# Inverse lengths and inverse roots moved from ScalarE and VectorE to a power on GpSimd, in the gate stage of a four-layer kernel

## The chip, the cores and the metric

The kernel runs on one core of a Trainium2 chip. The metric is device time in microseconds of one execution, in fp32. PE is TensorE, DVE VectorE, ACT ScalarE, POOL GpSimd, SP the engine that issues the transfers.

## The reference

The program is four layers of x = x + attention(n) * silu(gate(n)), with n the layer norm of x. The change touches the gate of layer 1, itself a small transformer of two layers on 2 x 1024 tokens of width 128, with 8 heads of 64 and a local window of 64 tokens:

```python
def l2norm(t):
    return t / jnp.clip(jnp.linalg.norm(t, axis=-1, keepdims=True), 1e-12)
...
def _layer(x, wqkv, qs, ksc, wo, lg, lb, w1, b1, w2, b2):
    h = shift_token(x)
    q, k, v = jnp.split(h @ wqkv, 3, axis=-1)
    ...
    q = l2norm(q) * qs
    k = l2norm(k) * ksc
    q, k = rotary_xpos(q, k)
    o = local_attention(q, k, v)
    ...
    x = x + o @ wo
    h = shift_token(x)
    mu = h.mean(-1, keepdims=True)
    var = h.var(-1, keepdims=True)
    h = (h - mu) / jnp.sqrt(var + 1e-05) * lg + lb
    h = h @ w1 + b1
    a, g = jnp.split(h, 2, axis=-1)
    h = a * jax.nn.gelu(g, approximate=False)
    x = x + h @ w2 + b2
    return x
```

The square roots in question are those of the lengths of q and k, one for each token and head, and of the variance, one for each token.

## The kernel before

The class TransformerGate treats the tokens in 8 units of 4 tiles of 128 tokens: units 0 to 3 are the first of the two layers, 4 to 7 the second. The work is cut into items, and `plan` puts each on a step: unit u has its attention on steps 8u to 8u+7, two steps to a tile, and its other items before and after. Inside a step the items stand by `rank`. Every engine walks the same list of items in that order and does its own part of each, so the list is the order of every engine's queue, and an instruction that waits holds up all that stands behind it on its engine.

What a unit does, by steps relative to its first: from -15 to -4 PE makes q, k and v (L1730); ACT squares q and k (L1910) and copies them (L1913), and DVE sums the squares of each head into F_ssq (L1964). At -7 `root` takes ACT's square root of F_ssq (L1865), and at -6 `lengths` runs `norms` on DVE (L2033 to L2039): two reciprocals and one refining step that turn 64 lengths of each token (4 tiles, q and k, 8 heads) into inverse lengths; for q, 8 times the inverse goes into the exponentials as a scale. From -8 to -1 POOL rotates the rows (`spin`, L2103 to L2108) in the order q0, q1, k0, k1, q2, k2, q3, k3; only the keys (L2103) need the inverse lengths first. From -4 to 2 PE turns each tile (`turn`, L1763), k and then q, and DVE copies the result (L2012, L2016); at step 2 POOL copies the last keys of the unit to the next one's place (L2081, or a memset at L2079), which in its queue stands between q1 and k0 of the next unit. Then scores, maxima (L2023, L2026), exponentials on ACT (L1923), the turn of the weights (L1789), the products with v (L1812), and the projection (L1821). ACT copies the turned denominators (`over`, L1855) for DVE (L1955).

The norm of a unit comes with step 9 (`moments`, DVE, to L2047; then `norm`, ACT's root at L1868, last of the step) and step 10 (`layernorm`, DVE, L2054 to L2061), and the feed-forward part with steps 11 to 14 (L1829, L1743, L1881 with Gelu, L1842). Step 9 of a unit is step -7 of the unit two further on, so the root of the norm and that of the lengths stand side by side on ACT. Square root, exponential and Gelu are in different tables of ACT, and a table load (ACT_TABLE_LOAD) stands before the first use after another.

Of the kernel before, what the change touches and what calls it, by code (L numbers as in the profile page):

```python
# [12 lines left out]
ALU = mybir.AluOpType  # L13
AX = mybir.AxisListType

P = 128
# [1484 lines left out]
class TransformerGate:  # L1501
# [17 lines left out]
    def __init__(self, core, ctx, io):  # L1519
# [6 lines left out]
        self.b1, self.lgb, self.gains = two("b1", [P, 2, 3]), two("lgb", [P, 2]), two("gains", [P, 2, 64])  # L1526
        self.mask, self.zero = sb("mask", [P, 2, 1, P], BF16), sb("zero", [P, 1])
        self.hT = two("hT", [P, BANK + 1])
        self.sq = [sb(f"sq{i}", [P, BANK]) for i in range(3)]
# [15 lines left out]
    def run(self):  # L1545
        core = self.core
        self.plan()
        (self.y_made, self.y_act, self.y_dve, self.squared, self.sq_summed, self.rooted, self.inverted, self.tab_made, self.spins, self.rotated, self.kcopied,
         self.s_made, self.nm_half, self.nm_made, self.expd, self.den_made, self.w_turned, self.w_copied, self.pv,
         self.stepped, self.var_made, self.ln_rooted, self.z_normed, self.gate_made, self.scaled, self.tab0, self.tab1, self.early0, self.early1, self.z0, self.z1) = core.sems(*(  # L1550
            "y_made y_act y_dve squared sq_summed rooted inverted tab_made spins rotated kcopied s_made nm_half nm_made expd den_made "
            "w_turned w_copied pv stepped var_made ln_rooted z_normed gate_made scaled tab0 tab1 early0 early1 z0 z1").split())
        self.tab_loaded, self.early_loaded, self.z_moved = (self.tab0, self.tab1), (self.early0, self.early1), (self.z0, self.z1)
        pe, dve, act, pool, sp = core.engines()
        self.sync(sp)
        self.tensor(pe)
        self.vector(dve)
        self.scalar(act)
        self.gpsimd(pool)
        core.end()  # L1560

    def ahead(self, dve, pool, sp):
# [20 lines left out]
        for x in (self.kT[0][:, :, 0:P], self.early[0][0:64, :], self.zero[:, :]):  # L1583
            pool.e.memset(x, 0.0).then_inc(filled, 1)
        dve.e.memset(self.u[64:P, 2, :], 1.0).then_inc(filled, 1)
        sp.wait_ge(loaded, load.n)
# [3 lines left out]
    def plan(self):  # L1590
        at = {}
        put = lambda s, *its: at.setdefault(s, []).extend(its)
        for u in range(self.UNITS):
            first = 8 * u
            for i in range(4):
                put(first + 2 * i + 2, ("join", u, i), ("shift", u, i))
                put(first + 2 * i + 3, ("stats", u, i))
            put(first - 16, ("turnx", u))
            for r, i, x in self.QKV:
                put(first + r, ("qkv", u, i, x))  # L1600
            put(first - 9, ("table", u))
            put(first - 7, ("root", u))
            put(first - 6, ("lengths", u))
            for r, i, x in self.SPINS:
                put(first + r, ("spin", u, i, x))
            for r, i in self.TURNS:
                put(first + r, ("turn", u, i, 1), ("turn", u, i, 0))
            put(first + 9, ("moments", u), ("norm", u))
            put(first + 10, ("layernorm", u))
            put(first + 11, ("zturn", u))  # L1610
            put(first + 12, *[("gate", u, j) for j in range(3)])
            put(first + 13, *[("up", u, j) for j in range(3)])
            put(first + 14, ("down", u))
        rank = {"turn": 0, "stats": 0, "moments": 1, "table": 3, "join": 4, "shift": 4, "layernorm": 4, "lengths": 4, "zturn": 4, "turnx": 5, "gate": 5, "spin": 6, "qkv": 7, "up": 8, "down": 8, "norm": 10, "root": 10}
        items = self.items = []
# [12 lines left out]
        for it in items:  # L1628
# [5 lines left out]
            if it[0] == "qkv" and it[3] < 2:  # L1634
                self.no[it] = self.sqs
                self.sqs += 1
            if it[0] == "root":
                self.no[it] = self.sqs
# [208 lines left out]
    def scalar(self, act):  # L1847
        for it in self.items:
# [9 lines left out]
            elif kind == "qkv":  # L1858
                self.qkv_act(act, it)
            elif kind == "root":  # L1860
                u = it[1]
                act.wait_ge(self.sq_summed, self.no[it])
                if u >= 2:
                    act.wait_ge(self.expd, 4 * (u - 1))
                act.e.activation(self.ssq[u % 2][:, 1, :, :, :], self.ssq[u % 2][:, 0, :, :, :], ACT.Sqrt).then_inc(self.rooted, 1)  # L1865
            elif kind == "norm":
                act.wait_ge(self.var_made, it[1] + 1)
                act.e.activation(self.rb[:, :], self.ra[:, :], ACT.Sqrt).then_inc(self.ln_rooted, 1)  # L1868
            elif kind == "zturn":
# [60 lines left out]
    def vector(self, dve):  # L1930
        self.chain = Chain(dve, self.stepped)
        for it in self.items:
# [25 lines left out]
            elif kind == "qkv" and it[3] < 2:  # L1958
# [5 lines left out]
                dve.e.tensor_reduce(self.ssq[u % 2][:, 0, i, x, :], self.sq[n % 3][:, :].rearrange("p (h d) -> p h d", h=self.HEADS), AX.X, ALU.add).then_inc(self.sq_summed, 1)  # L1964
            elif kind == "lengths":
                self.norms(dve, it[1])
            elif kind == "join":
# [59 lines left out]

    def norms(self, dve, u):

        A, B, C = (self.ssq[u % 2][:, i, :, :, :] for i in range(3))  # L2030
        chain = self.chain
        dve.wait_ge(self.rooted, u + 1)
        chain(dve.e.tensor_scalar(B, B, 1e-12, None, ALU.max))  # L2033
        chain(dve.e.reciprocal(C, B))
        chain(dve.e.tensor_tensor(C, C, A, ALU.mult))
        chain(dve.e.tensor_tensor(B, B, C, ALU.add))
        chain(dve.e.tensor_scalar(B, B, 0.5, 1e-12, ALU.mult, ALU.max))
        chain(dve.e.reciprocal(A, B))
        dve.e.tensor_scalar(C[:, :, 0, :], A[:, :, 0, :], 8.0, None, ALU.mult).then_inc(self.inverted, 1)  # L2039

    def moments(self, dve, u):
# [7 lines left out]
    def layernorm(self, dve, u):  # L2049
# [3 lines left out]
        dve.wait_ge(self.z_normed, 4 * u)  # L2053
        chain(dve.e.reciprocal(out, b))  # L2054
        chain(dve.e.tensor_tensor(b, out, out, ALU.mult))
        chain(dve.e.tensor_tensor(b, b, a, ALU.mult))
        chain(dve.e.tensor_scalar(b, b, -0.5, 1.5, ALU.mult, ALU.add))
        chain(dve.e.tensor_tensor(out, out, b, ALU.mult))
# [6 lines left out]
    def gpsimd(self, pool):  # L2065
        chain = Chain(pool, self.spins)
        for it in self.items:
            kind = it[0]
            if kind == "table":
                self.table(pool, it[1])  # L2070
            elif kind == "spin":
                self.spin(pool, chain, it)
            elif kind == "turn" and it[2:] == (3, 1) and it[1] < self.UNITS - 1:
                u = it[1]
                self.yread(pool, it)
                if u:
                    pool.wait_ge(self.s_made, 4 * (u - 1) + 1)
                if u == 3:
                    pool.e.memset(self.kT[0][:, :, 64:P], 0.0).then_inc(self.kcopied, 1)  # L2079
                else:  # L2080
                    pool.e.tensor_copy(self.kT[(u + 1) % 2][:, :, 64:P], self.kT[u % 2][:, :, 4 * P + 64:5 * P]).then_inc(self.kcopied, 1)  # L2081

    def table(self, pool, u):
# [698 lines left out]
```

## Time and profile before

| | |
|---|---|
| median of 3 runs | 5166.3 us (5165.3 to 5180.0) |
| the profiled execution | 5168.0 us |
| its span, first to last instruction | 5166.7 us |
| granted PE clock, mean | 0.944 |
| gate stage of layer 1 | from about 1158 to 1624 us |

Durations in the rows are from the profiled execution; the span lies 1.3 us under its time. The page gives means over the whole program; the views by stretch, by wait and in order of time are the ones for a stage. In a row of the timeline the first number is the start, the second the length, and the brackets say how long the engine was idle before and whom it waited for. Tile names have the class's prefix (F_ for this stage), without numbers of buffers.

### The profile page before, as it was taken

Reading aid. Unit: us, or ns where it says so; the run is one execution under the profiler, and the core shown is the slowest. Engines: PE = TensorE matmul, PEld = TensorE weight load, DVE = VectorE, ACT = ScalarE, POOL = GpSimd, SP = SyncE. Lnnn points to the kernel's source line nnn. Section 1 sums busy time; section 2 is a strip of 40 time slices with the busy share of each in tenths; the row PEclk is TensorE's granted clock in tenths of the full one; section 3 lists DMA queues with packets and bytes.
Section 4 is the critical chain, followed back from the end, with each engine's and each line's share of the span. In section 5 each row is a group of like instructions: output and inputs, shape, how many; then the busy total and the mean of one; then the engine's idle time right before and its main releaser. Section 6 shows DMA issues by size and latency. Waiting matters only on the chain. (4 is left out here: it accounts for less than half of the span.)

```text
span 5166.7 us, 68811 instructions
## 1 busy us (share of the span) xinstructions
PE 4541.0 (88%) x27376; PEld 2213.2 (43%) x27376; DVE 3154.0 (61%) x4176; ACT 2497.4 (48%) x3813; POOL 2316.0 (45%) x1323
## 2 busy tenths in 40 slices
PE   5999999987886777868799999987799999999997
PEld 3444444445654333323322222223455555555554
DVE  4656565636666777762377777844465655566563
ACT  2344444446663555542256666651244444444443
POOL 0455555558771677870100000000166666666674
PEclk8999999989997999989799999997899999999998
DMA  0000000011110000000000000000000000000000
GB/s 32 3 3 3 3 3 3 3 33 29 37 26 12 2 2 2 1 1 23 3 2 2 1 2 1 1 3 6 10 3 3 3 1 3 3 3 1 3 1 9
DMA packets 61954, 36.81 MB, mean 7 GB/s; under 512 B 36308, under 2 KB 53888, under 8 KB 61376
## 3 DMA queue, kind: packets, MB, share of 16 engines
q1 hardware_dynamic: 61632, 32.41, 2.5%
q8 instruction: 216, 3.54, 0.3%
q14 instruction: 106, 0.87, 0.1%
HBM read 22.03 MB, written 1.05 MB: 4 GB/s over the span
## 5 line engine op out<-in xcount | busy, mean ns | idle before, releaser
L793 DVE TENSOR_REDUCE L_part<-banks 128x2 f32<-128x1024 f32 (+2 forms) x1600 | 1882.2, 1190 | 988.1 <-PE banks L644 847.7
L778 ACT ACTIVATE L_weights<-banks 128x1024 f32<-128x1024 f32 (+1 forms) x1600 | 1579.8, 1000 | 1048.3 <-PE banks L676 835.6
L702 PE MATMUL banks<-L_weights,L_V 128*32 128x512 f32 (+3 forms) x6400 | 1497.3, 603 | 5.6 <-ACT L_weights L778 3.6
L1000 POOL TENSOR_TENSOR L_wsum<-L_wsum,L_weights 128x1024 f32<-128x1024 f32 (+1 forms) x448 | 983.4, 2195 | 55.8 <-ACT L_weights L778 3.1
L983 POOL TENSOR_TENSOR L_wsum<-L_wsum,L_two 128x1024 f32<-128x1024 f32 x240 | 570.3, 2376 | 854.9 <-DVE L_two L967 852.6
L702 PEld LDWEIGHTS banks<-L_weights,L_V 128*64 128x64 f32 (+1 forms) x6400 | 283.3, 123 | 459.4 <-issue 396.9
L676 PE MATMUL banks<-L_QH,L_KH 64*128 64x512 f32 (+3 forms) x1664 | 431.7, 453 | 18.1 <-issue 10.2
L2510 POOL MEMSET F_xr<- 128x16 f32 x1 | 0.1, 126 | 934.6 <-POOLq L97 934.6
L644 PE MATMUL banks<-L_KH,L_QH 64*128 64x512 f32 (+3 forms) x1664 | 371.1, 428 | 31.6 <-ACT L_weights L778 17.5
L676 PE MATMUL banks<-L_QL,L_KH 64*128 64x512 f32 (+3 forms) x1664 | 371.8, 382 | 0.0
L676 PE MATMUL banks<-L_QM,L_onesrow 64*128 64x512 f32 (+3 forms) x1664 | 371.1, 380 | 0.0
L676 PE MATMUL banks<-L_QH,L_KL 64*128 64x512 f32 (+3 forms) x1664 | 371.0, 381 | 0.0
L967 DVE TENSOR_TENSOR L_two<-L_weights 128x1024 f32<-128x1024 f32 x240 | 337.0, 1404 | 51.2 <-ACT L_weights L778 50.8
L921 ACT ACTIVATE L_divided<-banks,L_rec 128x128 f32<-128x128 f32 x640 | 182.5, 368 | 332.2 <-PE banks L712 332.2
L676 PEld LDWEIGHTS banks<-L_QH,L_KH 64*128 64x128 f32 x1664 | 189.6, 185 | 327.2 <-issue 209.1
L644 PE MATMUL banks<-L_K,L_Q 32*128 32x512 f32 x1024 | 260.6, 514 | 25.1 <-ACT L_weights L778 15.6
L676 PEld LDWEIGHTS banks<-L_Q,L_K 32*128 32x128 f32 x1024 | 95.1, 182 | 401.9 <-issue 339.7
L930 POOL TENSOR_TENSOR SACC<-SACC,L_divided 128x512 f32<-128x512 f32 x160 | 217.8, 1361 | 108.5 <-ACT L_divided L921 108.4
L676 PE MATMUL banks<-L_Q,L_K 32*128 32x512 f32 x1024 | 256.4, 497 | 1.5 <-DVE L_Q L1429 0.8
L995 POOL TENSOR_TENSOR L_wsum<-L_weights 128x1024 f32<-128x1024 f32 (+1 forms) x80 | 189.7, 2372 | 134.6 <-ACT L_weights L778 116.3
L644 PEld LDWEIGHTS banks<-L_KH,L_QH 64*128 64x128 f32 x1664 | 172.2, 185 | 162.2 <-ACT L_weights L778 114.0
L712 PEld LDWEIGHTS banks<-L_Wo,L_raw 64*128 64x128 f32 x1280 | 160.5, 194 | 134.9 <-issue 101.5
(446 smaller groups left out, 5914.3 us busy)
## 6 DMA issues: line engine op xcount, KB each, us to landing
F_early<-F_V SPq DMA_DIRECT2D x63, 128.0 KB, 2.3
F_tab<-xpos SPq DMA_DIRECT2D x8, 512.0 KB, 4.5
F_h<-L_ffn_h_w SPq DMA_DIRECT2D x2, 1024.0 KB, 8.1
F_wqkv<-L_ffn_wqkv SPq DMA_DIRECT2D x2, 768.0 KB
L_cos<-rope_cos SPq DMA_DIRECT2D x1, 1024.0 KB, 5.0
L_sin<-rope_sin SPq DMA_DIRECT2D x1, 1024.0 KB, 7.0
out<-X SPq DMA_DIRECT2D x1, 1024.0 KB, 5.1
F_z<-F_x SPq DMA_DIRECT2D x32, 31.8 KB
```

The costliest lines, as they stand in the source:

```text
L644: mm = pe.e.matmul(banks[:, x, 0:wide], q[:, a:a + P], k[:, p * KC:p * KC + wide], start=True, stop=not (on or self.cut(n, j, p)))
L676: mm = pe.e.matmul(S[:, y, c:BANK], k[:, kk] if k.shape[1] == T else k[:, :], q[:, a + c:a + BANK], start=t == 0, stop=t == len(terms) - 1 ...
L702: mm = pe.e.matmul(O[r, c:BANK], self.V[g % 2][:, kt, h, :], self.W[x % self.NW][:, y, c:BANK], start=kt < starts, stop=kt >= tiles - starts)
L712: mm = pe.e.matmul(Y[:, j * P:(j + 1) * P], self.raw[n % 2][r, j * P:(j + 1) * P], self.Wo[self.chunk[n][0] % 2][r, :], start=True, stop=True)
L778: act.e.activation(self.W[x % self.NW][:, :, c:BANK], self.banks(it)[:, :, c:BANK], ACT.Exp, scale=self.scale).then_inc(self.exped, 1)
L793: dve.e.tensor_reduce(self.part[n % 3][:, pr, j, p, :], self.banks(it)[:, :, 0:wide], AX.X, ALU.max).then_inc(self.mx_read, 1)
L921: last = act.e.activation(self.divided[h][:, j, :], self.ybanked(it)[:, j * P:(j + 1) * P], ACT.Copy, scale=self.rec[n % 2][:, h, j:j + 1])
L930: pool.e.tensor_tensor(acc, acc, self.divided[h][:, :, :], ALU.add).then_inc(self.merged, 1)
L967: dve.e.tensor_tensor(self.two[twos % 2][:, :, :], self.W[(x - 1) % self.NW][:, :, :], self.W[x % self.NW][:, :, :], ALU.add).then_inc(sel ...
L983: pool.e.tensor_tensor(acc[:, :, :], acc[:, :, :], self.two[twos % 2][:, :, :], ALU.add).then_inc(self.summed, 1)
L995: pool.e.tensor_tensor(acc[:, :, c:BANK], before[:, :, c:BANK], W[:, :, c:BANK], ALU.add).then_inc(self.summed, 1)
L1000: pool.e.tensor_tensor(acc[:, :, c:BANK], acc[:, :, c:BANK], W[:, :, c:BANK], ALU.add).then_inc(self.summed, 1)
```

## The change

The lengths' inverses are made on POOL: the sum of squares is bounded from below, raised to the power -0.5, refined by one step of Newton's, and for q multiplied by 8. They stand on step -7 behind q1 in POOL's queue, where ACT's root stood, and no longer on step -6. The norm's root becomes POOL's power too, on step 9 ahead of the rotations of that step (rank 4), that is ahead of q1 of the unit two further on; DVE's layernorm loses its reciprocal. ACT has no square root left in this class, and DVE no `norms`.

```diff
@@ -1525,6 +1525,7 @@
         self.w1, self.w2 = two("w1", [P, 2 * HID]), two("w2", [P, 3, P])
         self.b1, self.lgb, self.gains = two("b1", [P, 2, 3]), two("lgb", [P, 2]), two("gains", [P, 2, 64])
         self.mask, self.zero = sb("mask", [P, 2, 1, P], BF16), sb("zero", [P, 1])
+        self.minus = sb("minus", [P, 1])
         self.hT = two("hT", [P, BANK + 1])
         self.sq = [sb(f"sq{i}", [P, BANK]) for i in range(3)]
         self.rows = [[sb(f"{x}n{i}", [P, HEADS, 64]) for i in range(6)] for x in "qk"]
...
@@ -1582,6 +1583,7 @@
                         load(self.b1[l][0:n, half, j:j + 1], io["L1_ffn_b1"][l][half * HID + a:half * HID + a + n].rearrange("(p a) -> p a", a=1))
         for x in (self.kT[0][:, :, 0:P], self.early[0][0:64, :], self.zero[:, :]):
             pool.e.memset(x, 0.0).then_inc(filled, 1)
+        pool.e.memset(self.minus[:, :], -0.5).then_inc(filled, 1)
         dve.e.memset(self.u[64:P, 2, :], 1.0).then_inc(filled, 1)
         sp.wait_ge(loaded, load.n)
 
@@ -1599,19 +1601,18 @@
             for r, i, x in self.QKV:
                 put(first + r, ("qkv", u, i, x))
             put(first - 9, ("table", u))
-            put(first - 7, ("root", u))
-            put(first - 6, ("lengths", u))
+            put(first - 7, ("lengths", u))
             for r, i, x in self.SPINS:
                 put(first + r, ("spin", u, i, x))
             for r, i in self.TURNS:
                 put(first + r, ("turn", u, i, 1), ("turn", u, i, 0))
-            put(first + 9, ("moments", u), ("norm", u))
+            put(first + 9, ("moments", u), ("root", u))
             put(first + 10, ("layernorm", u))
             put(first + 11, ("zturn", u))
             put(first + 12, *[("gate", u, j) for j in range(3)])
             put(first + 13, *[("up", u, j) for j in range(3)])
             put(first + 14, ("down", u))
-        rank = {"turn": 0, "stats": 0, "moments": 1, "table": 3, "join": 4, "shift": 4, "layernorm": 4, "lengths": 4, "zturn": 4, "turnx": 5, "gate": 5, "spin": 6, "qkv": 7, "up": 8, "down": 8, "norm": 10, "root": 10}
+        rank = {"turn": 0, "stats": 0, "moments": 1, "table": 3, "join": 4, "shift": 4, "layernorm": 4, "root": 4, "zturn": 4, "turnx": 5, "gate": 5, "spin": 6, "lengths": 7, "qkv": 7, "up": 8, "down": 8}
         items = self.items = []
         whole = lambda w: 0 <= w < self.STEPS
         for s in range(min(at), max(at) + 1):
@@ -1634,7 +1635,7 @@
             if it[0] == "qkv" and it[3] < 2:
                 self.no[it] = self.sqs
                 self.sqs += 1
-            if it[0] == "root":
+            if it[0] == "lengths":
                 self.no[it] = self.sqs
             if it[0] == "spin":
                 self.no[it] = 8 * it[1] + self.SPINS.index(next(sp for sp in self.SPINS if sp[1:] == it[2:])) + 1
@@ -1857,15 +1858,6 @@
                 self.shifted_in(act, it)
             elif kind == "qkv":
                 self.qkv_act(act, it)
-            elif kind == "root":
-                u = it[1]
-                act.wait_ge(self.sq_summed, self.no[it])
-                if u >= 2:
-                    act.wait_ge(self.expd, 4 * (u - 1))
-                act.e.activation(self.ssq[u % 2][:, 1, :, :, :], self.ssq[u % 2][:, 0, :, :, :], ACT.Sqrt).then_inc(self.rooted, 1)
-            elif kind == "norm":
-                act.wait_ge(self.var_made, it[1] + 1)
-                act.e.activation(self.rb[:, :], self.ra[:, :], ACT.Sqrt).then_inc(self.ln_rooted, 1)
             elif kind == "zturn":
                 u = it[1]
                 self.ymade(act, it)
@@ -1962,8 +1954,6 @@
                 if u >= 2:
                     dve.wait_ge(self.expd, 4 * (u - 2))
                 dve.e.tensor_reduce(self.ssq[u % 2][:, 0, i, x, :], self.sq[n % 3][:, :].rearrange("p (h d) -> p h d", h=self.HEADS), AX.X, ALU.add).then_inc(self.sq_summed, 1)
-            elif kind == "lengths":
-                self.norms(dve, it[1])
             elif kind == "join":
                 u, i = it[1:]
                 self.ymade(dve, it)
@@ -2025,19 +2015,6 @@
         dve.wait_ge(self.inverted, u + 1)
         dve.e.tensor_tensor(nm[:, :], nm[:, :], self.ssq[u % 2][:, 2, i, 0, :], ALU.mult).then_inc(self.nm_made, 1)
 
-    def norms(self, dve, u):
-
-        A, B, C = (self.ssq[u % 2][:, i, :, :, :] for i in range(3))
-        chain = self.chain
-        dve.wait_ge(self.rooted, u + 1)
-        chain(dve.e.tensor_scalar(B, B, 1e-12, None, ALU.max))
-        chain(dve.e.reciprocal(C, B))
-        chain(dve.e.tensor_tensor(C, C, A, ALU.mult))
-        chain(dve.e.tensor_tensor(B, B, C, ALU.add))
-        chain(dve.e.tensor_scalar(B, B, 0.5, 1e-12, ALU.mult, ALU.max))
-        chain(dve.e.reciprocal(A, B))
-        dve.e.tensor_scalar(C[:, :, 0, :], A[:, :, 0, :], 8.0, None, ALU.mult).then_inc(self.inverted, 1)
-
     def moments(self, dve, u):
         chain = self.chain
         dve.wait_ge(self.stepped, chain.n)
@@ -2051,10 +2028,9 @@
         a, b, out = self.ra[:, :], self.rb[:, :], self.rstd[:, :]
         dve.wait_ge(self.ln_rooted, u + 1)
         dve.wait_ge(self.z_normed, 4 * u)
-        chain(dve.e.reciprocal(out, b))
-        chain(dve.e.tensor_tensor(b, out, out, ALU.mult))
-        chain(dve.e.tensor_tensor(b, b, a, ALU.mult))
-        chain(dve.e.tensor_scalar(b, b, -0.5, 1.5, ALU.mult, ALU.add))
+        chain(dve.e.tensor_tensor(out, b, b, ALU.mult))
+        chain(dve.e.tensor_tensor(out, out, a, ALU.mult))
+        chain(dve.e.tensor_scalar(out, out, -0.5, 1.5, ALU.mult, ALU.add))
         chain(dve.e.tensor_tensor(out, out, b, ALU.mult))
         z = self.z[u % 2]
         for i in range(4):
@@ -2070,6 +2046,11 @@
                 self.table(pool, it[1])
             elif kind == "spin":
                 self.spin(pool, chain, it)
+            elif kind == "lengths":
+                self.lengths(pool, chain, it)
+            elif kind == "root":
+                pool.wait_ge(self.var_made, it[1] + 1)
+                pool.e.tensor_tensor(self.rb[:, :], self.ra[:, :], self.minus[:, :].to_broadcast([P, 4]), ALU.pow).then_inc(self.ln_rooted, 1)
             elif kind == "turn" and it[2:] == (3, 1) and it[1] < self.UNITS - 1:
                 u = it[1]
                 self.yread(pool, it)
@@ -2079,6 +2060,22 @@
                     pool.e.memset(self.kT[0][:, :, 64:P], 0.0).then_inc(self.kcopied, 1)
                 else:
                     pool.e.tensor_copy(self.kT[(u + 1) % 2][:, :, 64:P], self.kT[u % 2][:, :, 4 * P + 64:5 * P]).then_inc(self.kcopied, 1)
+
+    def lengths(self, pool, chain, it):
+
+        u = it[1]
+        A, B, C = (self.ssq[u % 2][:, i, :, :, :].rearrange("p i x h -> p (i x h)") for i in range(3))
+        pool.wait_ge(self.sq_summed, self.no[it])
+        if u >= 2:
+            pool.wait_ge(self.expd, 4 * (u - 1))
+        chain(pool.e.tensor_scalar(A, A, 1e-24, None, ALU.max))
+        chain(pool.e.tensor_tensor(B, A, self.minus[:, :].to_broadcast([P, 64]), ALU.pow))
+        chain(pool.e.tensor_tensor(C, B, B, ALU.mult))
+        chain(pool.e.tensor_tensor(C, C, A, ALU.mult))
+        chain(pool.e.tensor_scalar(C, C, -0.5, 1.5, ALU.mult, ALU.add))
+        chain(pool.e.tensor_tensor(A, C, B, ALU.mult))
+        A, C = (self.ssq[u % 2][:, i, :, 0, :] for i in (0, 2))
+        pool.e.tensor_scalar(C, A, 8.0, None, ALU.mult).then_inc(self.inverted, 1)
 
     def table(self, pool, u):
```

## Rows read from the trace of the kernel before

**Rows 1.** The page, busy us of each engine (share of the span).

```profile
PE 4541.0 (88%) x27376; PEld 2213.2 (43%) x27376; DVE 3154.0 (61%) x4176; ACT 2497.4 (48%) x3813; POOL 2316.0 (45%) x1323
```

**Rows 2.** Windows: stretch, length, busy us of PE, PEld, DVE, ACT, POOL; clock, DMA.

```profile
1180.00:1260.00 80.00, 63.10 (x624) 44.14 (x625) 54.47 (x94) 54.34 (x159) 75.75 (x84) 0.91 0.12 33
...
1320.00:1375.00 55.00, 46.91 (x466) 33.33 (x466) 37.59 (x80) 37.38 (x104) 39.22 (x44) 0.94 0.13 33
```

**Rows 3.** Waits from 1140 to 1620 us: total us, times, longest.

```profile
PE banks L1763 <- POOL F_kn L2108: 45.6, 10, 6.9
...
POOL F_kn L2103 <- DVE F_ssq L2039: 43.7, 8, 6.7
```

**Rows 4.** Timeline 1352 to 1381 us: start, length, instruction, [idle before, releaser].

```profile
1356.77 0.73 POOL L2105 TENSOR_TENSOR F_rot<-F_qn,F_tab 128x256 f32<-128x256 f32 x1
...
1358.15 1.26 POOL L2107 TENSOR_TENSOR F_spun<-F_qn,F_tab 128x512 f32<-128x512 f32 x1
...
1359.49 1.33 POOL L2108 TENSOR_TENSOR F_qn<-F_spun,F_rot 128x512 f32<-128x512 f32 x1
...
1364.08 1.28 ACT L1868 ACT_TABLE_LOAD   x1
1364.34 0.17 DVE L2047 TENSOR_SCALAR F_ra<-F_mv 128x4 f32<-128x4 f32 x1
...
1366.48 1.28 ACT L1923 ACT_TABLE_LOAD   x1
...
1367.92 0.31 POOL L2079 MEMSET F_kT<- 128x256 f32 x1 [7.10 <-DVE F_kT L2012]
...
1374.68 0.18 DVE L2039 TENSOR_SCALAR F_ssq<-F_ssq 128x32 f32<-128x32 f32 x1
...
1374.94 1.04 POOL L2103 TENSOR_TENSOR F_kn<-F_kn,F_ssq 128x512 f32<-128x512 f32 x1 [6.71 <-DVE F_ssq L2039]
...
1380.17 1.09 PE L1763 MATMUL banks<-ident,F_kn 128*128 128x128 f32 x4 [4.69 <-POOL F_kn L2108]
```

**Rows 5.** Groups of lines of ACT, 1140 to 1625 us: busy us, mean ns.

```profile
L1923 ACT ACT_TABLE_LOAD x16 | 20.5, 1283 | 0.3
...
L1868 ACT ACT_TABLE_LOAD x8 | 10.3, 1283 | 0.1
```

**Rows 6.** Timeline of unit 0, DVE and POOL.

```profile
1176.07 0.69 DVE L1964 TENSOR_REDUCE F_ssq<-F_sq 128x8 f32<-128x512 f32 x1 [0.29 <-ACT F_sq L1910]
...
1179.49 1.04 POOL L2103 TENSOR_TENSOR F_kn<-F_kn,F_ssq 128x512 f32<-128x512 f32 x1 [5.01 <-DVE F_ssq L2039]
```

**Rows 7.** Groups by shape, POOL, whole span.

```profile
L2089 POOL TENSOR_TENSOR F_tab<-F_tab,F_gains 128x256 f32<-128x256 f32 x16 | 11.6, 725 | 15.4 <-DMA F_tab<-xpos 15.4
...
L2091 POOL TENSOR_TENSOR F_tab<-F_tab,F_gains 128x128 f32<-128x128 f32 x16 | 7.3, 454 | 0.0
...
L2081 POOL COPY F_kT<-F_kT 128x256 f32<-128x256 f32 x6 | 2.4, 397 | 23.2 <-DVE F_kT L2012 23.2
```

**Rows 8.** Groups by shape, DVE, 1140 to 1625 us.

```profile
L2034 DVE RECIPROCAL F_ssq<-F_ssq 128x64 f32<-128x64 f32 x8 | 4.4, 553 | 0.3
...
L2035 DVE TENSOR_TENSOR F_ssq<-F_ssq 128x64 f32<-128x64 f32 x8 | 2.3, 292 | 0.3
```

**Rows 9.** Timeline of units 1, 2 and 7, at k0.

```profile
1221.21 1.04 POOL L2103 TENSOR_TENSOR F_kn<-F_kn,F_ssq 128x512 f32<-128x512 f32 x1 [1.19 <-DVE F_ssq L2039]
...
1226.43 1.09 PE L1763 MATMUL banks<-ident,F_kn 128*128 128x128 f32 x4 [4.85 <-POOL F_kn L2108]
...
1266.05 1.04 POOL L2103 TENSOR_TENSOR F_kn<-F_kn,F_ssq 128x512 f32<-128x512 f32 x1 [4.32 <-DVE F_ssq L2039]
...
1523.94 0.17 DVE L2047 TENSOR_SCALAR F_ra<-F_mv 128x4 f32<-128x4 f32 x1
...
1533.46 1.04 POOL L2103 TENSOR_TENSOR F_kn<-F_kn,F_ssq 128x512 f32<-128x512 f32 x1 [6.63 <-DVE F_ssq L2039]
```

**Rows 10.** Timeline, ACT, near the stage's end.

```profile
1571.45 0.20 ACT L1868 ACTIVATE F_rb<-F_ra 128x4 f32<-128x4 f32 x1 [4.01 <-DVE F_ra L2047]
```

More of the change, by code:

```diff
@@ L1547, in run @@
         self.plan()
-        (self.y_made, self.y_act, self.y_dve, self.squared, self.sq_summed, self.rooted, self.inverted, self.tab_made, self.spins, self.rotated, self.kcopied,
+        (self.y_made, self.y_act, self.y_dve, self.squared, self.sq_summed, self.inverted, self.tab_made, self.spins, self.rotated, self.kcopied,
          self.s_made, self.nm_half, self.nm_made, self.expd, self.den_made, self.w_turned, self.w_copied, self.pv,
          self.stepped, self.var_made, self.ln_rooted, self.z_normed, self.gate_made, self.scaled, self.tab0, self.tab1, self.early0, self.early1, self.z0, self.z1) = core.sems(*(
-            "y_made y_act y_dve squared sq_summed rooted inverted tab_made spins rotated kcopied s_made nm_half nm_made expd den_made "
+            "y_made y_act y_dve squared sq_summed inverted tab_made spins rotated kcopied s_made nm_half nm_made expd den_made "
             "w_turned w_copied pv stepped var_made ln_rooted z_normed gate_made scaled tab0 tab1 early0 early1 z0 z1").split())
```

## The prediction

> **What bounds the kernel now.** The page comes first: PE is busy for 88% of the span and no other engine above 61% [rows 1], but these are means over the eight blocks of the program, and the diff touches one stage, the gate of layer 1, from about 1158 to 1624 us. So the rest is read from that stage by stretches. The reader should see two regimes there [rows 2]: in the first full units (1180 to 1260 us) POOL is busy 75.75 of 80 us and is the bound; in a later unit (1320 to 1375 us) PE is busy 46.9 of 55 us, POOL 39.2, ACT 37.4 and DVE 37.6, so nobody is full and a wait sets the pace. The view of waits names it [rows 3]: PE stood 45.6 us in ten waits for POOL's rotated keys (F_kn), and POOL stood 43.7 us in eight waits, one in each unit, for F_ssq, the inverse lengths that the change moves.
>
> The timeline of one unit shows how the two hang together [rows 4]. I call the first key tile of a unit k0, the second query tile q1. POOL ends q1 at 1360.82 and has nothing until DVE has copied the keys of the unit before (memset 1367.92, 7.10 us idle), then nothing until DVE comes to the lengths in its own order (end 1374.86, k0 starts 1374.94, 6.71 us idle). At 1380.17, 5.2 us after k0's start, PE starts the turn of k0, and has been idle for 4.69 us. So the end of the lengths sets k0, k0 sets PE's turn, and the turn sets the unit. Behind it everything has drained, so whatever the change saves or adds between the moments (DVE L2047, end 1364.51) and k0 counts one for one.
>
> **The change, part by part.**
>
> *Removed from ACT.* Sixteen square roots and the table loads that they cause: L1868's eight, and of L1923's sixteen the eight that follow a root (the others follow a Gelu, which stays): 16 x 1.283 = 20.5 us [rows 5]. On the path they are worth little: without the pair at 1364.08 and 1366.48 [rows 4] ACT copies the denominators and makes its exponentials earlier, but PE then only arrives earlier at the turn for which it waits 4.69 us. What covers this saving is that wait; without the cover it would be worth at most the 20.5 us.
> The Trainium skill (ScalarE: Activation LUTs, What ACT_TABLE_LOAD costs) charges 1283 ns for the load and about 1380 ns more for a drain; by that, an estimate, 16 switches would free 43 us. The trace agrees with the first figure only: the load at 1364.08 is followed by the next load at 1366.48 with two roots and a copy of 512 columns between, which leaves no room for a drain.
>
> *Removed from DVE.* Seven instructions in each unit, from L2033 to L2039; with ACT's root ahead of them they take 2.73 us in unit 0, from the last sum (end 1176.76) to k0 at 1179.49 [rows 6]. The norm loses one reciprocal. DVE is idle at these places; only the latency counts.
>
> *Added to POOL, lengths (L).* Three tensor-tensor operations, three tensor-scalar ones and the power, on 64 elements (the last on 32). POOL's price from two sizes [rows 7]: 454 ns at 128 elements and 725 at 256, so 2.1 ns per element and 0.18 us fixed; 0.32 us at 64. One input is cheaper (the copy of 256 elements takes 397 ns, so some 0.23 us at 64). The six plain ones are 3 x 0.32 + 3 x 0.23 = 1.65 us, and the gap between two chained ones is 0.08 us (1358.15 + 1.26 to 1359.49) [rows 4], six times 0.5: 2.15 us. L = 2.15 + X, X being the power.
> The power on POOL is in no row. Below it can't cost less than a plain tensor-tensor: 0.32 us. It is a logarithm, a product and an exponential; DVE's reciprocal, one step away from plain arithmetic, takes 553 ns where its tensor-tensor takes 292 [rows 8], which excludes that unusual functions are free on these engines. My estimate is 20 elementary steps at the 2.1 ns per element of the multiply: 0.18 + 20 x 0.135 = 2.9; I take X = 3.0. The far end is 60 such steps, 8.3 us.
>
> *Added to POOL, the norm's root (R).* The same power on 4 elements: nearly fixed cost, 0.2 to 1 us; I take 0.4. It is put ahead of q1, and waits for the moments of the unit two behind. Behind it on POOL stand q1, the lengths, the key copy and k0. Today q1 (4.05 us) runs before the moments are there, in time that is then idle [rows 4]; now it comes after them. DVE wants the root only in its layernorm at about 1370, five us later than POOL would have it, so no new wait on DVE.
>
> *The sum.* k0 would start after the moments by a hop of 0.1, R, q1 with its gap 4.1, L, and the key copy with gaps 0.5: 4.7 + R + L. Today it is 10.43 us in the unit shown [rows 4] and 9.35 in the last, unit 7 (1524.11 to 1533.46) [rows 9]; for the five units 3 to 7 I take 10.4. The moves of k0 are
> - unit 0: L - 2.7 (the sums are its start today and after);
> - unit 1: POOL was full and stood only 1.19 us ahead of k0 (1221.21) [rows 9]; L takes the place of that wait, but for 0.1 of hops: L - 1.1. PE stood 4.85 us for this k0 (1226.43), so it counts;
> - unit 2: POOL stood 4.32 us ahead of k0 (1266.05): R + L - 4.2;
> - units 3 to 7: five times R + L - 5.7;
> - the end of the stage: ACT's copy no longer stands behind a root that waits 4.01 us for the moments [rows 10], but DVE, which wants the copy, makes the moments first anyway, so only the root, its hops and the reciprocal go: -1.2.
>
> Together 8L + 6R - 37.7 = 8X + 6R - 20.5. With X = 3.0 and R = 0.4 this is 24.0 + 2.4 - 20.5 = +5.9 us. Against the profiled execution (5166.7 span, 5168.0 in all) that is 5173.9; the median of the runs is 1.7 lower, 5166.3, so **5172** there. Ends: X = 0.32, R = 0.2 gives -16.7 (5150), X = 8.3, R = 1 gives +52 (5218).
>
> **Rivals.** A change under 0.3% (15.5 us) is about what a measurement of this kernel can't tell from none.
> (A) *The power is slow.* Its steps depend on each other, and POOL can't overlap them. From X of about 4.2 on the kernel is slower by more than 15.5 us. At 45 steps' worth, X = 6.3, it is +32: 5199. For it: nothing in the program uses a function beyond add and multiply on POOL. Against it: 4.2 us is already 30 steps of the plain price. The Trainium skill (GPSIMD Engine Reference, Performance pitfalls for Q7 kernels) says that a dependent fp32 chain costs 4 cycles per element and step; no run shows it yet.
> (B) *The power is nearly plain* (X = 0.4, R = 0.2): -16: 5150, faster. It decides from X below 0.45. For it: POOL's small operations are cheap here. Against it: the reciprocal's price on DVE.
> (C) *The table loads are on the path after all*, because PE's wait at the turn is not for POOL alone: all 20.5 us come back and the sum is 5.9 - 20.5 = -14.6: 5152, at the edge of faster. Against it: in the unit shown the release is F_kn, and PE's arrival is 4.69 us too early already.
> (D) *POOL becomes the bound.* Its work of 39.2 us per unit grows by R + L to about 45, still under the 53 to 55 us of a unit; only with X above 11 does it decide. It is the same side as A.
>
> **How the numbers follow.** Forecast (X from 0.45 to 4.2) 0.46; A and D together 0.39; B 0.11; C 0.04, half of it faster. So faster 0.13, same 0.48, slower 0.39. The likeliest case alone holds 5151 to 5182. Since both sides hold much, the range reaches to the low end of B, 5150, and into A up to X = 7.5 (+42): 5208; what is left out is some 0.05 below and 0.1 above.
>
> **What would show it.** In the profile after: no ACT_TABLE_LOAD at roots, eight left at exponentials and eight at Gelu; the power's duration at 64 elements (3 us) and at 4 (0.4); k0 right behind the key copy with no wait for F_ssq; a new POOL wait for F_ra in place of the 7.1 us wait; k0 at 4.7 + R + L after the moments; PE still idle at the turn of k0, longer than 4.69 us in the middle units. A power under 0.4 or above 4.2 us makes the forecast wrong by its term; a k0 that starts early while the time doesn't follow would show that PE's turn isn't what sets the unit.

## The result, and the profile after

The changed kernel takes 5244.4 us (median of 5, 5236.58 to 5248.03) against 5168.8 (5165.31 to 5179.99) of the kernel before: ratio 1.014, interval 1.0123 to 1.0156, slower by 1.4%. The profiled execution took 5243.2 us with a span of 5241.8, which is 75.1 us over the span before. The forecast was 5172 with a range from 5150 to 5208.

The page after, which answers to [rows 1]. PE's busy time has hardly moved (4541.0 before) and POOL has 111 us more.

```profile
PE 4555.5 (87%) x27376; PEld 2220.7 (42%) x27376; DVE 3125.8 (60%) x4112; ACT 2471.9 (47%) x3780; POOL 2427.0 (46%) x1388
```

To see where the 75.1 us arose I cut the span at two marks on POOL: the first memset of F_kT, where the gate's program begins, and the casts of L_KB behind the gate. First the timeline of the kernel before, then that of the kernel after.

```profile
1139.86 0.52 POOL L1584 MEMSET F_kT<- 128x512 f32 x1 [0.50 <-POOLq L97]
...
1627.18 6.12 POOL L1230 CAST L_KB<-L_weights 32x512 fp32r<-32x512 f32 x8 [64.73 <-DVE L_weights L1219]
```

```profile
1144.84 0.53 POOL L1585 MEMSET F_kT<- 128x512 f32 x1 [0.50 <-POOLq L97]
...
1700.11 6.12 POOL L1230 CAST L_KB<-L_weights 32x512 fp32r<-32x512 f32 x8 [20.86 <-DVE L_weights L1219]
```

Between the marks lie 487.32 us before and 555.27 after: the stage has grown by 67.9 us. Another 5.0 us arose ahead of the first mark and 2.2 behind the second, where both kernels do the same. I use this stage length for all kernels below. The part behind the second mark, which no edit touches, takes 3538 to 3546 us in seven of the thirteen profiled executions and 3550 to 3552 in the other six, so whole times carry a difference of some 12 us that comes from no edit.

The operations on F_ssq and F_rb, all of the kernel after (columns: duration in ns, least, median, greatest; first and last start):

```profile
L2071 POOL TENSOR_SCALAR F_ssq<-F_ssq x8: 368/404/435, 1179.5 to 1594.6; 128x64 f32<-128x64 f32 x8
L2072 POOL TENSOR_TENSOR F_ssq<-F_ssq,F_minus x8: 10553/10555/10561, 1179.9 to 1595.1; 128x64 f32<-128x64 f32 x8
L2073 POOL TENSOR_TENSOR F_ssq<-F_ssq x8: 292/292/293, 1190.6 to 1605.7; 128x64 f32<-128x64 f32 x8
...
L2053 POOL TENSOR_TENSOR F_rb<-F_ra,F_minus x8: 1007/1032/1037, 1282.3 to 1678.2; 128x4 f32<-128x4 f32 x8
```

The main cause stands in these four rows. A plain tensor-tensor on 64 elements takes 0.29 us, the power on the same 64 elements takes 10.56 us, and on 4 elements 1.03.

The waits after, from 1140 to 1700 us, answer to [rows 3]:

```profile
PE banks L1764 <- POOL F_kn L2105: 116.1, 10, 18.2
DVE F_kT L2002 <- PE banks L1764: 107.6, 9, 18.2
...
POOL F_rb L2053 <- DVE F_ra L2024: 74.4, 7, 31.0
```

PE's wait for the rotated keys has grown from 45.6 to 116.1 us, in ten waits as before: that is 70.5 us, about the growth of the stage (67.9). POOL's wait for F_ssq is gone, and the new one for the variance (F_ra) has come.

One unit on POOL, after, answers to [rows 4]; the last row is PE's turn of k0.

```profile
1343.51 1.03 POOL L2053 TENSOR_TENSOR F_rb<-F_ra,F_minus 128x4 f32<-128x4 f32 x1 [6.59 <-DVE F_ra L2024]
1344.52 0.72 POOL L2102 TENSOR_TENSOR F_rot<-F_qn,F_tab 128x256 f32<-128x256 f32 x1
...
1348.58 0.43 POOL L2071 TENSOR_SCALAR F_ssq<-F_ssq 128x64 f32<-128x64 f32 x1
1349.10 10.55 POOL L2072 TENSOR_TENSOR F_ssq<-F_ssq,F_minus 128x64 f32<-128x64 f32 x1
...
1361.60 0.40 POOL L2062 COPY F_kT<-F_kT 128x256 f32<-128x256 f32 x1
1361.96 1.04 POOL L2100 TENSOR_TENSOR F_kn<-F_kn,F_ssq 128x512 f32<-128x512 f32 x1
...
1367.18 1.08 PE L1764 MATMUL banks<-ident,F_kn 128*128 128x128 f32 x4 [13.13 <-POOL F_kn L2105]
```

The reader should see an unbroken chain on POOL from the variance to k0: norm's root, q1, the lengths with the power in their midst, the key copy, k0. It takes 18.45 us, where the old way took 10.4. PE stands 13.13 us before the turn where it stood 4.69.

Windows of one unit each, from k0 to k0, before and after (columns as in [rows 2]):

```profile
1320.44:1374.94 54.50, 46.41 (x452) 32.83 (x448) 37.13 (x78) 36.88 (x102) 39.15 (x43) 0.94 0.13 33
```

```profile
1361.96:1423.67 61.71, 46.20 (x444) 32.70 (x444) 34.79 (x69) 33.74 (x97) 52.48 (x52) 0.89 0.12 29
```

PE is busy as long as before (46.2 against 46.4 us); the 7.2 us by which the unit is longer are idle time. POOL is busy for 52.5 of 61.7 us, so in this unit it is not the bound by its load, it is late in the chain. The first units are another case. Here is the stretch of [rows 2] that holds them, after:

```profile
1180.00:1260.00 80.00, 43.20 (x365) 27.55 (x364) 30.65 (x49) 33.57 (x98) 76.78 (x70) 0.79 0.07 18
```

From k0 of unit 0 to that of unit 1 POOL is busy for 51.24 of 53.42 us, and to that of unit 2 for 52.81 of 54.85: there it is the bound, and the power adds to a queue that is full. In the unit of the two windows above, the granted clock has sunk from 0.94 to 0.89 without a cost in PE's busy time here.

### The profile page after: what moved, and what is told of

Same layout as the page of the kernel before. It is cut to its first block and busy times, and to the rows that moved or that the text cites. A ratio compares the mean times of both kernels' runs of the same rounds, so it can differ in the third digit from the quotient of the medians.

```text
span 5241.8 us, 68807 instructions
## 1 busy us (share of the span) xinstructions
PE 4555.5 (87%) x27376; PEld 2220.7 (42%) x27376; DVE 3125.8 (60%) x4112; ACT 2471.9 (47%) x3780; POOL 2427.0 (46%) x1388
```

## The experiments

Each ratio is against runs of the kernel before on the same chip, interval in brackets. The stage length is that between the two marks, from the profiled execution.

| kernel | what it is | ratio | stage, us (against 487.3) |
|---|---|---|---|
| after | the change | 1.0140 [1.0123, 1.0156] | 555.3 (+67.9) |
| e1_mult | the power replaced by a multiply | 0.9970 [0.9957, 0.9984] | 473.0 (-14.3) |
| e2_norm | only the norm's root on POOL | 0.9998 [0.9985, 1.0010] | 485.4 (-2.0) |
| e3_lengths | only the lengths on POOL | 1.0049 [1.0032, 1.0067] | 518.1 (+30.8) |
| e8_early | the change, lengths a step earlier | 1.0063 [1.0041, 1.0086] | 521.1 (+33.8) |
| e5_halves | the power in two instructions | one run, 5246.5 us | 555.3 (+68.0) |
| v1_rank | before, lengths ahead of layernorm | 1.0030 [1.0020, 1.0039] | 500.2 (+12.9) |
| v2_norm | Newton's steps on DVE for the lengths | 1.0018 [1.0009, 1.0028] | 487.8 (+0.4) |
| v2_dve | the same for both, no roots at all | 1.0034 [1.0022, 1.0046] | 506.5 (+19.2) |
| v1_wait | v1_rank and one wait more | 0.9977 [0.9967, 0.9987] | 476.2 (-11.1) |
| v3_norm | v2_norm and that wait | 0.9987 [0.9976, 0.9999] | 473.6 (-13.7) |
| v3_dve | v2_dve and that wait | 1.0001 [0.9990, 1.0013] | 483.2 (-4.1) |

**e1_mult: is it the power alone?** Everything of the change stays, but the power of the lengths is a multiply by 1e-6, so the inverse lengths of this kernel are not the reference's.

```diff
-        chain(pool.e.tensor_tensor(B, A, self.minus[:, :].to_broadcast([P, 64]), ALU.pow))
+        chain(pool.e.tensor_tensor(B, A, self.small[:, :].to_broadcast([P, 64]), ALU.mult))
```

> The changed kernel with one edit: the power of the 64 sums of squares on POOL is a multiplication by a small constant, so the inverse lengths are not those of the reference; everything else, the norm's power on 4 elements too, stays. Theory 1, the price of the power (10.56 us a unit in the trace of the changed kernel): the multiplication costs 0.32 us, eight times 10.2 us go, and the time is 5244 - 82 = 5162 us, or 5157 by the sum of the prediction with X = 0.32 and R = 1.03. Theory 2, the order: what costs is that POOL now waits for the moments ahead of q1; the time stays above 5200 us. Theory 3, the table loads were never on the path; it gives no number of its own here, but below 5150 us would speak against it.

Measured 5162.8 us, ratio 0.997, and a stage of 473.0, that is 82.2 us less than after. Eight powers less eight multiplies of 0.295 us are 8 x 10.26 = 82.1. So the power's time counts one for one, and all the rest of the change (order, waits, roots gone from ACT) makes the kernel faster by some 14 to 16 us. The prediction's formula, with X = 0.295 and R = 1.03, gives 2.4 + 6.2 - 20.5 = -11.9.

**e5_halves: is the power's price per instruction or per element?** The power is cut in two instructions of 32 elements.

```diff
-        chain(pool.e.tensor_tensor(B, A, self.minus[:, :].to_broadcast([P, 64]), ALU.pow))
+        chain.step(pool.e.tensor_tensor(B[:, 0:32], A[:, 0:32], self.minus[:, :].to_broadcast([P, 32]), ALU.pow))
+        chain(pool.e.tensor_tensor(B[:, 32:64], A[:, 32:64], self.minus[:, :].to_broadcast([P, 32]), ALU.pow))
```

> The changed kernel with the power of 64 elements made in two instructions of 32. A fixed part of 0.40 us and 158.7 ns per element, as the rows at 4 and 64 elements give: 5.48 us each, 10.96 us in all, the span 3 us longer than that of the changed kernel. If the price is not linear in elements (a start-up of its own, or a dependence on values), the two don't come to 5.48 us.

```profile
L2072 POOL TENSOR_TENSOR F_ssq<-F_ssq,F_minus x8: 5446/5450/5457, 1174.7 to 1589.6; 128x32 f32<-128x32 f32 x8
L2073 POOL TENSOR_TENSOR F_ssq<-F_ssq,F_minus x8: 5410/5416/5421, 1180.1 to 1595.0; 128x32 f32<-128x32 f32 x8
```

From 4 and 64 elements: (10.555 - 1.032) / 60 = 0.1587 us per element and 0.40 us fixed, which gives 5.48 us at 32; the rows have 5.45 and 5.42. The price is linear in the elements. The 3 us that were expected on top are not to be seen in the stage (555.3 as after), but nothing is won by cutting either, and the power would have to be spread over fewer columns, which here are all needed.

**e2_norm and e3_lengths: each half alone.** e2_norm leaves the lengths with ACT's root and DVE, and has POOL take the norm's root ahead of q1. e3_lengths has the lengths on POOL and the norm's root on ACT.

The edit of e2_norm against the kernel before:

```diff
-                act.wait_ge(self.var_made, it[1] + 1)
-                act.e.activation(self.rb[:, :], self.ra[:, :], ACT.Sqrt).then_inc(self.ln_rooted, 1)
+                pool.wait_ge(self.var_made, it[1] + 1)
+                pool.e.tensor_tensor(self.rb[:, :], self.ra[:, :], self.minus[:, :].to_broadcast([P, 4]), ALU.pow).then_inc(self.ln_rooted, 1)
```

> The kernel before with the norm's part alone: the root of the norm is POOL's power on 4 elements ahead of q1, the lengths stay with ACT's root and DVE. Theory 1: POOL waits for the moments, then 1.0 us of power and 4.1 us of q1 end 5.2 us after the moments, and the lengths come from DVE at 10.4 us as before, so k0 doesn't move: 5169 us, within 6. Theory 2, the wait for the moments in POOL's queue costs by itself: 5 units of 5 us, 5190 us or more.

> The changed kernel with the lengths' part alone: the norm's root is ACT's again, as before, and POOL doesn't wait for the moments. Theory 1: L = 13 us, but in units 3 to 7 it runs in the 5 to 7 us that POOL stood ahead of the key copy and in the 6.6 us that it stood for the lengths, so those units gain or lose about nothing; units 0 to 2 lose 10.3, 11.9 and 8.7 us: 5200 us. A rival by which each of the eight lengths costs its 10 us wherever it stands: 5240 us. The table loads come back with the norm: where they matter, 20 us on top.

e2_norm measures 0.9998: the norm's root, though it holds q1 back until the moments, costs nothing by itself, since POOL is idle behind q1 in that order. e3_lengths measures 1.0049, some 25 us, and a stage 30.8 us longer: a third to a half of the loss with the same power eight times. By the starts of k0, 28.4 of the 30.8 us arise up to unit 2, where POOL has little idle time to hide the power in (30.9 were expected), and 2.4 in units 3 to 7. There POOL runs q1 and the power before the moments are there, in the idle time of [rows 4]. Together the halves lose 68 us in the stage, apart 31 and none: by the timeline of one unit above it is the chain of variance, root, q1, power and k0 that makes the rest, and either half alone lacks a link of it.

**e8_early: the change with the lengths a step earlier**, so that the power stands ahead of the norm's root and q1.

```diff
-            put(first - 7, ("lengths", u))
+            put(first - 8, ("lengths", u))
```

> The changed kernel with the lengths one step earlier, so that in POOL's queue they stand behind q0 and ahead of the norm's root and q1. Theory 1: in units 3 to 7 they fill the 6.6 us in which POOL stands for the moments, and k0 comes 6.6 us earlier each time, while unit 0 loses 4 us since q1 now follows: 5244 - 29 = 5215 us. If POOL's total work is the bound already (39.2 + 14.4 = 53.6 us a unit), nothing moves: 5240 us.

Measured 1.0063, stage +33.8. Half of the loss was the place. By the starts of k0, 31.2 us of what is left arise up to unit 2, where POOL was nearly full before, and 5.3 in units 3 to 7, which had lost 39.8 in the changed kernel (the end of the stage gives 2.7 back). In a unit of these POOL is busy for 52.58 of 54.64 us: with this order POOL is the bound, the case that the prediction kept as rival D.

```profile
1353.84:1408.48 54.64, 45.51 (x444) 31.38 (x444) 39.31 (x71) 33.79 (x97) 52.58 (x53) 0.91 0.13 32
```

Something else is in this kernel too. DVE's last step of the layernorm (F_z) takes 753 ns in the mean, where it takes 342 in the kernel before, and PE waits 47.8 us for what comes of it, where it waited 4.6:

```profile
L2037 DVE TENSOR_SCALAR F_z<-F_z,F_mv,F_rstd 128x128 f32<-128x128 f32 x32 | 22.1, 753 | 0.3
...
PE banks L1830 <- DVE F_x L1960: 47.8, 5, 15.6
```

What that costs on top of POOL's load no run separates. The next runs show where it comes from.

**v2_norm, v2_dve and v1_rank: k0 earlier without the power.** If k0 sets the unit, anything that brings the lengths forward should win. v2_norm makes the lengths on DVE from an integer first guess and three steps of Newton's, one step earlier in the order, with no root (13 instructions, 3.2 us); v2_dve makes the norm's root in the same way too; v1_rank only lets DVE make the lengths ahead of the layernorm.

The lengths of v2_norm on DVE, and behind it the one edit of v1_rank, in plan:

```diff
+        chain(q.e.tensor_scalar(out.bitcast(I32), a.bitcast(I32), -0.5, float(0x5F3759DF), ALU.mult, ALU.add))
+        for _ in range(3):
+            chain(q.e.scalar_tensor_tensor(t, out, -0.5, out, ALU.mult, ALU.mult))
+            chain(q.e.tensor_tensor(t, t, a, ALU.mult))
+            chain(q.e.scalar_tensor_tensor(out, t, 1.5, out, ALU.add, ALU.mult))
...
-"layernorm": 4, "lengths": 4,
+"layernorm": 4, "lengths": 2,
```

> The same for the lengths, but the norm's root is ACT's as before, so one pair of table loads (2.57 us) a unit comes back. The table loads had a cover, PE's wait for k0; here the cover is gone. If they stay off the path: the time of v2_dve, or up to 8 us less, since DVE's norm is 1 us shorter. If they are on the path once the cover is gone: 10 to 20 us slower than v2_dve.

> No square root, no power and no POOL for either part: DVE makes a first guess of the inverse root from the bits of the number (one multiply-add on the integer view) and refines it by three steps of Newton's, 10 small instructions; the lengths stand on step -8, behind the last sums, the norm's in the layernorm. Theory 1 (the end of the lengths sets k0, k0 sets PE's turn): k0 starts right behind the key copy, PE's wait of 4.7 us at the turn goes in units 3 to 7 with about 1 us of slow clock behind each, unit 1 gains 1.2 and unit 2 4.3 us: some 34 us, ratio to the kernel before 0.9935, 5140 us. Rival: something else is due at the same time (the FFN matmuls, POOL's 39 us of rotations), and less than 10 us comes back: 0.998 or more.

> The kernel before with one number changed: DVE makes the lengths ahead of the layernorm and the join of the step (rank 2), not behind them. Theory 1: lengths and k0 2.4 us earlier in units 3 to 7, the layernorm as much later, where PE has 4.7 us to spare: 5 x 2.4 = 12 us less, ratio 0.9977. Rival: the turn of z (PE, behind the layernorm) holds PE up by the same 2.3 us, and nothing is gained: 1.000.

All three missed: ratios of 1.0018, 1.0034 and 1.0030 where a gain was expected. The waits of v1_rank (total, times, longest) show that PE's wait had moved to the turn of z, which the rival of v1_rank had named with a smaller price. First the wait for F_x in the kernel before, then the waits of v1_rank:

```profile
PE banks L1829 <- DVE F_x L1970: 4.6, 5, 1.7
```

```profile
PE banks L1829 <- DVE F_x L1970: 41.6, 5, 9.7
...
PE banks L1763 <- POOL F_kn L2108: 13.7, 5, 6.9
```

And the timeline of v1_rank says why:

```profile
1379.43 1.04 POOL L2103 TENSOR_TENSOR F_kn<-F_kn,F_ssq 128x512 f32<-128x512 f32 x1 [4.25 <-DVE F_ssq L2039]
1379.46 1.03 DVE L2055 TENSOR_TENSOR F_rb<-F_rstd 128x4 f32<-128x4 f32 x1
...
1381.91 1.26 POOL L2107 TENSOR_TENSOR F_spun<-F_kn,F_tab 128x512 f32<-128x512 f32 x1
1382.01 4.38 DVE L2061 TENSOR_SCALAR F_z<-F_z,F_mv,F_rstd 128x128 f32<-128x128 f32 x4
...
1386.64 1.11 PE L1829 MATMUL banks<-ident,F_z 128*128 128x128 f32 x4 [7.98 <-DVE F_x L1970]
```

The same instructions of DVE in the kernel before, where POOL is idle from 1368.23 to 1374.94:

```profile
1370.28 0.16 DVE L2055 TENSOR_TENSOR F_rb<-F_rstd 128x4 f32<-128x4 f32 x1
...
1371.07 1.12 DVE L2061 TENSOR_SCALAR F_z<-F_z,F_mv,F_rstd 128x128 f32<-128x128 f32 x4
```

In v1_rank DVE's product on 4 elements starts right behind POOL's product on 512, takes 1.03 us in place of 0.16, and ends at 1380.49, with POOL's at 1380.47. The four z instructions take 4.38 us in place of 1.12. So these instructions of DVE stand still while POOL's are at the memory. In the kernel before DVE makes its layernorm while POOL waits for the lengths: the idle 6.71 us of [rows 4] that I took for pure loss sheltered the layernorm. The Trainium skill (GPSIMD Engine Reference, Specifications) says that GpSimd shares its memory interfaces with VectorE, with contention for VectorE's instructions in a two-port mode or with two inputs from SBUF. For two inputs the timeline of v2_norm agrees (the z instructions have one tensor as input, and in which mode they run no row says):

```profile
1370.27 0.93 POOL L2109 TENSOR_TENSOR F_rot<-F_kn,F_tab 128x256 f32<-128x256 f32 x1
...
1370.52 0.17 DVE L2036 RECIPROCAL F_rstd<-F_rb 128x4 f32<-128x4 f32 x1
...
1371.15 1.27 POOL L2110 TENSOR_TENSOR F_spun<-F_kn,F_tab 128x512 f32<-128x512 f32 x1
...
1371.24 1.19 DVE L2038 TENSOR_TENSOR F_rb<-F_rb,F_ra 128x4 f32<-128x4 f32 x1
```

The reciprocal, with one input, runs inside POOL's product in 0.17 us; the product of two inputs ends at 1372.43, with POOL's at 1372.42.

**v1_wait, v3_norm and v3_dve: the same three with the shelter back.** POOL waits for the layernorm before k0:

```diff
+        if (i, x) == (0, 1) and u >= 2:
+            pool.wait_ge(self.z_normed, 4 * (u - 1))
```

> Kernel v1_rank (kernel before, the lengths ranked ahead of the layernorm on VectorE) with the same wait. GpSimd then starts k0 behind the layernorm, at about the time of the kernel before, and VectorE does the same work in another order. Theory 1 (contention cost v1_rank its 0.3%): F_z TENSOR_SCALAR back from 952 ns to 0.34 us and a ratio of 0.999 to 1.001. Theory 2 (the order did): it stays at 1.002 to 1.004.

> Kernel v2_norm (lengths on VectorE by an integer guess and three Newton steps, norm's root on ScalarE) with one wait more: GpSimd starts k0's rotation of unit u only when the layernorm of unit u-2 is through. Theory 1 (v2_norm lost because VectorE's layernorm ran beside GpSimd's rotation and stretched from 1.1 us to 3.7 us for its four z instructions, so that PE waited at z's turn, 28.0 us over 5 waits in place of 45.6 over 10 at k0's turn): the F_z TENSOR_SCALAR mean falls from 828 ns back to about 0.34 us, the wait of PE for F_x is gone, k0 starts at about 1372 to 1373 against 1374.94 in the kernel before, and the time is 10 to 20 us below the kernel before: ratio 0.996 to 0.998. Theory 2 (the order of VectorE's work, not the contention, cost the time): GpSimd's wait only adds delay, ratio 1.002 to 1.004.

> Kernel v2_dve (no root and no power at all) with the same wait of GpSimd for the layernorm of two units before. Theory 1: F_z TENSOR_SCALAR back to 0.34 us from 649 ns, ratio 0.996 to 0.999; the seven or so instructions that the norm's root takes on VectorE stand ahead of the layernorm in the same step, so it is at most as fast as v3_norm. Theory 2: 1.003 to 1.005.

The z instructions, grouped by shape (busy us, mean ns): first the row of v1_rank, then that of v1_wait.

```profile
L2061 DVE TENSOR_SCALAR F_z<-F_z,F_mv,F_rstd 128x128 f32<-128x128 f32 x32 | 28.6, 952 | 0.3
```

```profile
L2061 DVE TENSOR_SCALAR F_z<-F_z,F_mv,F_rstd 128x128 f32<-128x128 f32 x32 | 8.9, 342 | 0.3
```

A wait added makes each of the three faster: 1.0030 to 0.9977, 1.0018 to 0.9987, 1.0034 to 1.0001, and the mean of the z instructions is 342 ns in all three (952, 828 and 649 without it). That shows that contention, not DVE's order, had cost the time. v1_wait did better than I expected (0.999 to 1.001), v3_norm and v3_dve did less well (0.996 to 0.998 and 0.996 to 0.999). One unit of v1_wait:

```profile
1318.07:1369.18 51.11, 43.66 (x444) 30.08 (x444) 38.42 (x78) 36.81 (x101) 38.97 (x43) 1.00 0.14 35
```

Against the unit before (54.50 us, PE busy 46.41, clock 0.94) PE has 2.75 us less to do at a full clock. Over the four units from there, 204.95 us against 213.02, PE's busy time is 176.76 against 180.08 and its idle time 28.19 against 32.94: some 5 of the 8 us are shorter waits, and 3 are busy time at a higher granted clock (0.97 to 1.00 in these units against 0.93 to 0.97). In the unit before PE stood 4.69 us ahead of k0's turn, and the four transposes behind it took 1.09 us; the same four with no such idle time ahead take 0.66. First that row of the kernel before, then two of v1_wait:

```profile
1363.85 0.66 PE L1763 MATMUL banks<-ident,F_kn 128*128 128x128 f32 x4
```

```profile
1323.33 0.63 PE L1763 MATMUL banks<-ident,F_kn 128*128 128x128 f32 x4 [2.05 <-POOL F_kn L2110]
...
1374.44 1.09 PE L1763 MATMUL banks<-ident,F_kn 128*128 128x128 f32 x4 [2.05 <-POOL F_kn L2110]
```

In the four units of v1_wait PE waits 2.05 us or less at k0's turn; three of the four turns take 0.63 us and one still takes 1.09. So a shorter wait of PE gives back some clock, but not each time. v1_wait, which changes one rank and adds one wait, beats the kernel before, and with e1_mult out of the question it is the fastest of these kernels by its ratio. v3_norm has a stage shorter by 2.6 us but a ratio that is not better. Its profiled execution gains 12.4 us on that of the kernel before, near the 13.7 of its stage, while that of v1_wait gains 11.1 in the stage and loses 12.6 behind the second mark, where both kernels do the same. So the ratios don't rank these two; why the part behind the mark differs was not found.

## Why the prediction was wrong

**The step that failed is the term X**, the power's duration. The prediction took 3.0 us (20 elementary steps at POOL's plain price) and called 60 steps, 8.3 us, the far end; it is 10.56 us. The nearest row, DVE's reciprocal at 1.9 times its tensor-tensor, is no guide to POOL's power, which is 36 times the tensor-tensor of the same size there. The bound was an estimate with nothing above it to hold it, and the range stopped even short of that bound (X = 7.5). R was 1.03 us where 0.4 was taken and 1 was the far end.
The rule of the Trainium skill that was set against the plain price (GPSIMD Engine Reference, Performance pitfalls for Q7 kernels), a dependent chain that is charged per element and step, pointed the right way, to a power dearer than the plain price. That the price is linear in the elements (e5_halves) fits both and doesn't tell them apart. How many steps the power has no run shows.

**The sum was right.** With X = 10.555 and R = 1.03 the formula 8X + 6R - 20.5 gives 84.4 + 6.2 - 20.5 = +70.1 us; the stage grew by 67.9. Unit by unit, by the starts of k0, less the 5.0 us by which the stage began later (L = 2.15 + X = 12.7; measured in the timeline of unit 0 12.98):

| | predicted | measured |
|---|---|---|
| unit 0 | L - 2.7 = 10.0 | 1192.47 - 1179.49 - 4.98 = 8.0 |
| unit 1 | L - 1.1 = 11.6 | 53.42 - 41.72 = 11.7 |
| unit 2 | R + L - 4.2 = 9.5 | 54.85 - 44.84 = 10.0 |
| units 3 to 7 | 5 x (R + L - 5.7) = 40.2 | 307.21 - 267.41 = 39.8 |
| end | -1.2 | 67.9 - 69.5 = -1.6 |

Only unit 0 is off by more than a microsecond: the prediction let the chain of this unit start at the last sum, as it does before, and that premise was wrong. In its new place the chain no longer stands behind the next unit's first squares, and starts at 1179.49, straight behind q1 (end 1179.40).

**Table loads.** The forecast was that sixteen loads go, and are worth nothing behind PE's wait. Groups of ACT after:

```profile
L1915 ACT ACT_TABLE_LOAD x8 | 10.3, 1283 | 0.1
...
L1873 ACT ACT_TABLE_LOAD x8 | 10.3, 1283 | 0.1
```

Eight at the exponentials and eight at Gelu are left, as said; 17 are gone, one more than was counted (one stood at L1865, ahead of the lengths of unit 1). That they are worth little is borne out by the changed kernel itself and by e1_mult, where they are gone too: the stages are 2.2 and 2.4 us shorter than the formula gives without any gain of theirs, and in the changed kernel 2.0 of that are unit 0's. e2_norm says nothing of it, since the root of the lengths keeps the loads (15 at exponentials and 7 at roots are left there). v2_dve and v3_dve, without a root, are not faster than v2_norm and v3_norm, which keep the norm's eight (stages of 506.5 against 487.8 and 483.2 against 473.6): the loads that they save are worth less than what DVE's added instructions cost. Rival C is excluded as a gain of 20.5 us.

**Waits.** k0 right behind the key copy, no wait for F_ssq, a new wait for F_ra, PE idle longer than 4.69 us at k0's turn: all four are in the rows. Of the rivals A was the right one, beyond its own price: it put X at 6.3. D did not come about in the later units of the change (POOL busy for 85% of the one shown), but in its first ones, where POOL was nearly full before (96% from k0 of unit 0 to that of unit 2), and in e8_early (96%). There the sum had the price right all the same, since it charged L in full.

**What the prediction did not see** is that "whatever the change saves or adds between the moments" and k0 "counts one for one" need not hold for a gain. For the loss it is confirmed to 2 us. It also read DVE as idle at the places of the seven instructions; in the unit of [rows 4] DVE works without a gap from 1366.57 to the end of the lengths, and its layernorm stands right ahead of them. A gain made in another way (v1_rank, v2_norm, v2_dve) ran into the contention with the layernorm. In e1_mult the earlier k0 did not, and its gain came in full: there the mean of the z instructions is 362 ns.

## What to carry to other kernels

Before a function is moved to another engine, measure it there at two sizes; a price from the engine's adds and multiplies says nothing of a power, and a bound that is only imagined is no end of a range. An engine's idle time beside another engine's work may be a shelter, as POOL's was for the layernorm: see which instructions run in it, and how long they take elsewhere in the trace when both engines work. A wait added at the right place can pay: here it turned three losses of 0.2 to 0.3% into two small gains and a tie.

## What the runs showed of the hardware

POOL's power in fp32 takes 0.40 us and 158.7 ns per element of the free size on 128 partitions (1.03 us at 4, 5.45 at 32, 10.56 at 64), where its tensor-tensor takes 0.29 us at 64.

DVE's instructions that stand still beside POOL's adds and multiplies don't do so beside its power. In the kernel after, the layernorm from 1349.13 on runs inside the power that starts at 1349.10 and takes 10.55 us, and is as fast as with POOL idle (0.16 us for a product of two inputs, 1.11 for the four z instructions; only its first instruction there, a tensor-scalar on 4, takes 0.29 in place of 0.17), while the copy just ahead, beside POOL's last addition of q1, takes 1.03 us in place of 0.43:

```profile
1347.75 1.03 DVE L1940 COPY F_wide<-F_rden 128x512 f32<-128x512 f32 x1
...
1349.45 0.16 DVE L2034 TENSOR_TENSOR F_rstd<-F_rstd,F_rb 128x4 f32<-128x4 f32 x1
...
1349.65 1.11 DVE L2037 TENSOR_SCALAR F_z<-F_z,F_mv,F_rstd 128x128 f32<-128x128 f32 x4
```

So it is not POOL's being busy that holds DVE up: a power on 64 elements did not in 10.55 us, products and sums on 512 did.
